# Gathering two graph attentions through rings of eight buffers in place of four, with GpSimd's run-out rounded up to whole rings

## The reference

```
e = leaky_relu(a_src[src] + a_dst[dst], 0.2)
ee = exp(e - segment_max(e, dst)[dst])
alpha = ee / (segment_sum(ee, dst)[dst] + 1e-16)
agg = segment_sum(h[src] * alpha, dst) + b_gat      # then layer norm, top 2 of 4, experts
```

```
h = x @ W;  a_src = (h * att_src).sum(-1);  a_dst = (h * att_dst).sum(-1)
e = leaky_relu(a_src[src] + a_dst[dst], 0.2)
alpha = softmax of e over the edges of one target
x = x + relu(segment_sum(h[src] * alpha, dst) + bias)
x = x + moe(layernorm(x))
```

## Time and profile before

| | |
|---|---|
| median of 3 runs | 5790.37 us (5789.03 to 5790.59) |
| the profiled execution | 5781.05 us, its span 5779.6 us |
| mean granted TensorE clock | 0.797 of full speed |
| busy: PE, DVE, ACT, POOL | 50%, 55%, 28%, 38% of the span |
| stage l1a | about 2215 to 3055 us of the span |
| stage l3a | about 4155 to 5780 us of the span |

### The profile page before, as it was taken

The page is one execution under the profiler, slowest core; times in us unless marked ns, Lnnn a source line. Parts: engine busy times, 40 slices in busy tenths (PEclk is TensorE's granted clock), DMA queues, the critical chain, the costliest instruction groups (busy, mean ns, idle before and its releaser), DMA issues. The chain is left out here.

```text
span 5779.6 us, 67813 instructions
## 1 busy us (share of the span) xinstructions
PE 2908.9 (50%) x15435; PEld 2113.2 (37%) x15474; DVE 3171.6 (55%) x7705; ACT 1642.9 (28%) x2993; POOL 2183.8 (38%) x2146
## 2 busy tenths in 40 slices
PE   0430065895995952566730489958301132343446
PEld 0320064784884841344520234446200111122224
DVE  8876386674776561222224554442455656676663
ACT  0322042773771211223310254322101222222221
POOL 1036212001001526566562100015366656666662
PEclk9999999997996975777865799979655566666678
DMA  0311154543433211111113634432323322332210
GB/s 29 68 32 31 8 195 159 170 131 117 133 95 106 66 57 41 21 25 25 30 23 99 233 128 159 167 98 65 127 71 82 80 68 70 82 79 78 65 43 23
DMA packets 332190, 488.33 MB, mean 84 GB/s; under 512 B 159589, under 2 KB 250259, under 8 KB 330134
## 3 DMA queue, kind: packets, MB, share of 16 engines
q1 hardware_dynamic: 192198, 269.65, 14.9%
q0 software_dynamic: 92304, 177.29, 11.8%
q10 hardware_dynamic: 47552, 39.98, 2.1%
HBM read 375.91 MB, written 137.24 MB: 89 GB/s over the span
## 5 line engine op out<-in xcount | busy, mean ns | idle before, releaser
L2253 POOL DMA_INDIRECT l3a_got<-rows,l3a_idx x928 | 976.6, 1052 | 528.4 <-issue 286.9
L2348 PE MATMUL ps<-l3a_xt,l3a_w 128*128 128x512 f32 (+1 forms) x448 | 268.8, 761 | 739.8 <-ACT l3a_h L2292 492.0
L2652 POOL DMA_INDIRECT l1a_got<-rows,l1a_idx x512 | 510.4, 997 | 318.5 <-issue 159.5
L1581 PE MATMUL ps<-l0a_all_rows,l0a_w 128*128 128x257 f32 x2500 | 556.5, 382 | 28.2 <-DVE l0a_w L1699 28.2
L1581 PEld LDWEIGHTS ps<-l0a_all_rows,l0a_w 128*128 128x128 f32 x2500 | 475.8, 191 | 101.7 <-issue 31.9
L1972 PE MATMUL ps<-l2a_table,l2a_count 128*128 128x512 bf16 x1837 | 411.3, 384 | 61.1 <-DVEq L2067 59.1
L2348 PEld LDWEIGHTS ps<-l3a_xt,l3a_w 128*128 128x128 f32 x448 | 112.0, 276 | 875.6 <-issue 875.4
L2277 ACT ACT_TABLE_LOAD x99 | 127.0, 1283 | 904.5 <-DVEq L2419 583.4
L2686 PE MATMUL ps<-l1a_w,l1a_h 128*128 128x256 f32 x800 | 232.3, 432 | 224.1 <-issue 168.3
L1972 PEld LDWEIGHTS ps<-l2a_table,l2a_count 128*128 128x128 bf16 x1875 | 185.2, 99 | 287.5 <-issue 72.1
L1508 ACT ACTIVATE l0a_low<-ps,l0a_factors x650 | 254.1, 509 | 86.7 <-PE ps L1571 79.1
(11 more groups left out here) (965 smaller groups left out, 6576.1 us busy)
## 6 DMA issues: line engine op xcount, KB each, us to landing
l0a_held<-counts SPq DMA_DIRECT2D x130, 640.0 KB
counts<-count_held SPq DMA_DIRECT2D x13, 3200.0 KB, 9.7
l2a_held<-counts SPq DMA_DIRECT2D x65, 640.0 KB
l3a_got<-rows,l3a_idx POOLq DMA_INDIRECT x928
l_y<-l1a_y_sb ACTq DMA_DIRECT2D x20, 640.0 KB
l2a_table<-rows SPq DMA_DIRECT2D x16, 640.0 KB
l2a_state<-l2a_seen SPq DMA_DIRECT2D x1, 9984.0 KB
l2a_seen<-l2a_state POOLq DMA_DIRECT2D x12, 768.0 KB, 6.0
```

Source lines behind the costliest of these rows:

```text
L1581: ins = pe.matmul(sums_of(n, k, D + 1), w[:, at, k * P:(k + 1) * P], all_rows[:, at, 1:RW], start=(at == 0), stop=False)
L2253: pool.indirect_dma_start(out=got[:, at:at + RW], out_offset=None, in_=rows[:, :], in_offset=bass.IndirectOffsetOnAxis(ap=idx[:, a, k:k + ...
L2348: ins = pe.matmul(ps[:, m, 0:size * P], w1[:, x, k, m * P:(m + 1) * P], xt[:, 0:size, k, :], start=(k == 0), stop=(k == KT - 1))
L2652: pool.indirect_dma_start(out=got[:, at:at + RW], out_offset=None, in_=rows[:, :], in_offset=bass.IndirectOffsetOnAxis(ap=idx[:, a, k:k + ...
```

## The change

`BUFFERS = 4` becomes `RING = 8` in both stages. The two loops run `(total + 7) // 8` times: 14 in l3a (112 blocks, 896 gathers in place of 928) and 8 in l1a (64 blocks as before). The padding behind a table becomes 16 blocks, written by two DMAs. The core of the diff (the same replacements are made in l1a, L2580 to L2656 and L2768):

```
-BUFFERS = 4
+RING = 8
...
-                    total = sp.value_load(s.base_row[0:1, NT:NT + 1], min_val=1, max_val=s.blocks - NT - 2 * SLOTS)
-                    sp.dma_start(s.table[bass.ds(total * (P * SLOTS), P * WIDE), 0].rearrange("(p s) -> p s", s=WIDE), empty[:, :]).then_inc(s.padded, 16)
+                    total = sp.value_load(s.base_row[0:1, NT:NT + 1], min_val=1, max_val=s.blocks - NT - 3 * SLOTS)
+                    for k in range(2):
+                        sp.dma_start(s.table[bass.ds((total + k * SLOTS) * (P * SLOTS), P * WIDE), 0].rearrange("(p s) -> p s", s=WIDE),
+                                     empty[:, :]).then_inc(s.padded, 16)
...
-                    sp.wait_ge(s.padded, 16)
+                    sp.wait_ge(s.padded, 32)
...
-                for a in range(BUFFERS):
+                for a in range(RING):
                     load(a, a)
...
-                with sp.Fori(0, (total + BUFFERS) // BUFFERS) as q:
-                    for a in range(BUFFERS):
+                with sp.Fori(0, (total + (RING - 1)) // RING) as q:
+                    for a in range(RING):
 
                         when(sp, c, gathered[a], (q + 1) * (16 * SLOTS))
                         sp.sem_inc(arrived, 1)
-                        load(q * BUFFERS + (BUFFERS + a), a)
+                        load(q * RING + (RING + a), a)
...
-                with pool.Fori(0, (total + BUFFERS) // BUFFERS) as q:
-                    for a in range(BUFFERS):
+                with pool.Fori(0, (total + (RING - 1)) // RING) as q:
+                    for a in range(RING):
 
                         when(pool, c, idx_in[a], (q + 1) * 16)
-                        when(pool, c, valued, q * (2 * BUFFERS) + (2 * a + 2))
+                        when(pool, c, valued, q * (2 * RING) + (2 * a + 2))
...
-                for a in range(BUFFERS):
+                for a in range(RING):
                     ch(dve.memset(buffer(a), FLOOR))
                     dve.sem_inc(valued, 2)
...
-                    when(dve, c, valued, b * 2 + 2 * BUFFERS)
+                    when(dve, c, valued, b * 2 + 2 * RING)
```

More of the change, by code:

```diff
@@ L2158, in attend_heads_beside_experts @@
         chain_sem, loaded, weights_in, arrived = (sem(n) for n in ("chain", "loaded", "weights_in", "arrived"))
-        idx_in = [sem(f"idx_in_{a}") for a in range(BUFFERS)]
-        gathered = [sem(f"got_{a}") for a in range(BUFFERS)]
+        idx_in = [sem(f"idx_in_{a}") for a in range(RING)]
+        gathered = [sem(f"got_{a}") for a in range(RING)]
         shifted, exped, weighed, valued = (sem(n) for n in ("shifted", "exped", "weighed", "valued"))
@@ L2205, in attend_heads_beside_experts @@
         first_of = lambda g, size: 0 if size == 1 else (g - 1) * G + 1
-        buffer = lambda b: got[:, bass.ds((b % BUFFERS) * (SLOTS * RW), SLOTS * RW)].rearrange("p (s w) -> p s w", w=RW)
+        buffer = lambda b: got[:, bass.ds((b % RING) * (SLOTS * RW), SLOTS * RW)].rearrange("p (s w) -> p s w", w=RW)
         valued_of = lambda b: v[:, bass.ds((b % 2) * (SLOTS * VW), SLOTS * VW)].rearrange("p (s h d) -> p s h d", h=H, d=DH + 1)
@@ L2214, in _ @@
             def _(sp):
-                total = sp.value_load(base_row[0:1, c.NT:c.NT + 1], min_val=1, max_val=blocks - 2 * BUFFERS)
+                total = sp.value_load(base_row[0:1, c.NT:c.NT + 1], min_val=1, max_val=blocks - 2 * RING)
                 def load(b, a):
@@ L2231, in _ @@
                     sp.dma_start(b2[:, :], b_out).then_inc(weights_in, 16)
-                with sp.Fori(0, (total + BUFFERS) // BUFFERS) as q:
-                    for a in range(BUFFERS):
+                with sp.Fori(0, (total + (RING - 1)) // RING) as q:
+                    for a in range(RING):
                         when(sp, c, gathered[a], (q + 1) * (16 * SLOTS))
                         sp.sem_inc(arrived, 1)
-                        load(q * BUFFERS + (BUFFERS + a), a)
-                for a in range(BUFFERS):
-                    when(sp, c, idx_in[a], ((total + BUFFERS) // BUFFERS + 1) * 16)
+                        load(q * RING + (RING + a), a)
+                for a in range(RING):
+                    when(sp, c, idx_in[a], ((total + (RING - 1)) // RING + 1) * 16)
             @block.gpsimd
             def _(pool):
-                total = pool.value_load(base_row[0:1, c.NT:c.NT + 1], min_val=1, max_val=blocks - 2 * BUFFERS)
+                total = pool.value_load(base_row[0:1, c.NT:c.NT + 1], min_val=1, max_val=blocks - 2 * RING)
                 last_node = pool.to_reg(c.N - 1)
-                with pool.Fori(0, (total + BUFFERS) // BUFFERS) as q:
-                    for a in range(BUFFERS):
+                with pool.Fori(0, (total + (RING - 1)) // RING) as q:
+                    for a in range(RING):
                         when(pool, c, idx_in[a], (q + 1) * 16)
-                        when(pool, c, valued, q * (2 * BUFFERS) + (2 * a + 2))
+                        when(pool, c, valued, q * (2 * RING) + (2 * a + 2))
                         for k in range(SLOTS):
@@ L2642, in _ @@
             def _(pool):
-                total = pool.value_load(base_row[0:1, c.NT:c.NT + 1], min_val=1, max_val=blocks - 2 * BUFFERS)
+                total = pool.value_load(base_row[0:1, c.NT:c.NT + 1], min_val=1, max_val=blocks - 2 * RING)
                 last_node = pool.to_reg(c.N - 1)
-                with pool.Fori(0, (total + BUFFERS) // BUFFERS) as q:
-                    for a in range(BUFFERS):
+                with pool.Fori(0, (total + (RING - 1)) // RING) as q:
+                    for a in range(RING):
                         when(pool, c, idx_in[a], (q + 1) * 16)
-                        when(pool, c, freed, q * BUFFERS + (a + 1))
+                        when(pool, c, freed, q * RING + (a + 1))
                         for k in range(SLOTS):
@@ L2765, in _ @@
                 dve.sem_inc(self_free, 2)
-                dve.sem_inc(freed, BUFFERS)
+                dve.sem_inc(freed, RING)
                 dve.sem_inc(emptied, 1)
```

12 lines of the change are left out of this document (6 added, 6 removed).

## The result

The changed kernel took 5893.52 us (5872.36 to 5899.75, 4 runs) against 5790.34 (5789.03 to 5790.59) on the same chip: a ratio of 1.0175, with a 95% interval of 1.0152 to 1.0198. It is 103 us slower. The profiled executions are 5892.2 and 5781.05 us, 111 us apart. The prediction had said 5804, with a range of 5745 to 5842.

What follows compares the result with a forecast made beforehand. DVE, slow while POOL issues without a stop, was taken to bound l3a. Terms 38 + 30 + 2 + 2 + 1 - 37 - 22 = +14 us gave 5795 on the profiled 5781.05, 5804 as median; range 5745 to 5842.

Steps and rivals of the forecast that it cites:

- What bounds the kernel: Both rings: POOL waits for DVE, 233.8 us in l3a and 158.6 in l1a; DVE, with two speeds, bounds l3a.
- slow after some 25 us of issue: Both stages: DVE's steps lengthen once POOL has issued indirect DMAs some 25 us without a stop, until POOL stops.
- Steady state of both rings: nothing.: Both rings once full: DVE's freeing of buffers still sets POOL's starts, so eight buffers change the time by nothing.
- First fill of l3a: Start of l3a: POOL runs eight blocks ahead, not four, with DVE slow meanwhile; +38 us taken.
- the worst pace: First fill of l3a at 24.5 us a block: POOL resumes at 4325.4, +43 us.
- the milder +28: First fill of l3a at 18.3 us a block: POOL stops for block 9 at 4337, +28 us.
- First fill of l1a: Start of l1a: at 21 us a block POOL stops for block 17, +33 us; +30 taken, +34 at 30 us.
- Index loads and padding: Stage starts: four more index loads, +2 us each in l3a and l1a; second padding DMA before table building, +1.
- The ends: Ends of l3a and l1a: last real blocks issued earlier, no dead gathers in l3a; -37 and -22 us.
- it is nothing: Rival, whole kernel: fills and ends cancel or are hidden, +5 us of loads, 5795 us; chance 0.10.
- More buffers feed DVE: Rival, l3a: POOL's stops delay DVE, so its 78.0 us of waits would go, 5717 us; chance 0.03.

Runs made afterwards that it cites:

- four_slow_dve: Kernel before with ring of four and the new run-out, plus six unread DVE memsets in each block of l3a: 5728.7 us.
- eight_slow_dve: Changed kernel with ring of eight, plus six unread DVE memsets in each block of l3a: 5739.41 us.
- four_exact: Kernel before, ring of four in both stages, only the run-out rounded as in the change: 5327.39 us, ratio 0.9994.
- after_again: The changed kernel itself, unedited, on later chips beside the kernel before: 5324.82 us, ratio 0.9999; once more 5327.87 us.
- eight_ahead2: Changed kernel, but POOL at most two blocks ahead of DVE in both stages; against the kernel before 5480.2 us, ratio 1.0289.
- eight_ahead3: Changed kernel, but POOL at most three blocks ahead of DVE in both stages; against the kernel before 5330.58 us, ratio 1.0002.
- the two kernels with pauses: Changed kernel, four blocks ahead, POOL waiting for its own gathers after every second block: 5512.32 us, ratio 1.0353; the text describes only this one.

## Why the prediction was wrong

**What bounds the kernel: right for the first chip, and for it alone.** The stops of POOL, DVE's two speeds and the ready rows were read rightly there. Later DVE has one speed, and POOL waits for it 24.5 us with four buffers and not at all with eight. The prediction took the condition of one measurement for a property of the kernel; nothing in one trace could tell them apart, but it gave no chance to it. Even in that trace its rule, slow after some 25 us of issue, doesn't always hold: 35 us from 5072.24 on pass without a slow block.

**The step that failed: "Steady state of both rings: nothing."** On the first chip the lag grew by 27 us in l1a and 50 in l3a behind the fills. The reasoning (once the ring is full, the same DVE times release POOL) is sound where DVE's times don't depend on POOL's runs: four_slow_dve and eight_slow_dve keep their distance over 112 blocks, to 1.5 us. With slow steps they do depend on them, and the longer fill leaves POOL's runs at another place of DVE's tiles. In l1a the rhythm can be read from POOL's stops, before and after:

```profile
2480.37 0.99 POOL L2652 DMA_INDIRECT l1a_got<-rows,l1a_idx  x1 [6.37 <-DVEq L2819]
2517.70 0.99 POOL L2652 DMA_INDIRECT l1a_got<-rows,l1a_idx  x1 [6.42 <-DVEq L2819]
```

```profile
2427.08 1.00 POOL L2654 DMA_INDIRECT l1a_got<-rows,l1a_idx  x1 [10.35 <-DVEq L2821]
2468.35 0.99 POOL L2654 DMA_INDIRECT l1a_got<-rows,l1a_idx  x1 [10.28 <-DVEq L2821]
```

Three blocks take 37.3 us before and 41.3 after, with the same 31 us of POOL and a stop of 10.3 in place of 6.4. That the place of the runs is the reason is argued from these rows, not shown by a run: no later chip had the slow steps. In l3a not even the rhythm was read, and with executions of the changed kernel up to 27 us apart a part of both drifts may belong to the recorded one alone. The cause of the drifts stays open.

**First fill of l3a: right.** +38 was taken, +36 measured; blocks at 23 to 26 us as at "the worst seen", and POOL goes on at 4378.63, 164 us behind its first gather, where the working at the worst pace had 4325.4 less 4161.5, also 164. So the working at the worst pace, +43, is the one that came out. That the +38 taken, between it and the milder +28, meets the +36 at block 9 is luck in part, since the lag behind the start was +53 at block 7.

**First fill of l1a: mis-sized.** +30 was taken, +34 was the upper bound, about +52 measured (+54 with the start's +2). The sum took 21 us for a block and let POOL stop for block 17. POOL stopped for block 14, and only one block further in DVE's work than before, 59 us behind the 2326.31 of the earlier trace rows: that one block took 49.8 us (2330.92 to 2380.67). The sum priced DVE's own steps and left out that DVE waits for TensorE in a block, whose single matmuls stand 2 to 3.5 us apart; 41.02 of the 49.8 us are such a wait, though its last 11 stand behind the last matmul and no record explains them.

**Index loads and padding:** +2, +2 and +1 predicted; 5 us are what the kernel with eight lags at block 0 of eight_slow_dve. Right in the sum.

**The ends: right.** -37 and -22 predicted, -33 and -25 measured, and the idle time of 25.11 us before L2540 is gone. On the other chips the dead gathers are hidden: four_exact gives 4 us, within what can't be told from none.

The lags of the table add up to -4 + 54 + 27 - 25 + 6 + 36 + 50 - 33 = +111, as they must. The two drifts, 77 us, and 22 of the first fill of l1a are the distance to the forecast of +14. Of the rivals, "it is nothing" gives the right time on the two later chips where the changed kernel ran, though not for its reason: there are no fills to pay. "More buffers feed DVE" has a true core there, since DVE does wait for gathers, but it waits for POOL's pace and not for a buffer, which no ring mends. The rule of the Trainium skill (SBUF — State Buffer, Practical consequences) that a DMA never contends with a compute engine fits the trace of after_again: POOL issues for 1220 us without a stop, and DVE's blocks that wait for nothing take the 7.9 us of the fast stretches. The first chip's traces differ from it as far as DVE's pace goes, whatever the reason.

**What stays open.** Why the first chip had slow steps: steps of 0.7 us and one recorded update in 0.7 us go together there, but a higher rate did nothing on another chip. Whether the recording itself makes the steps slow, and so whether they are in an execution that isn't recorded; this rival is untested. Whether it is the chip or the occasion. And whether a shorter ring or broken runs would help there: eight_ahead2, eight_ahead3 and the two kernels with pauses never met them.

## What to carry to other kernels

Before buying depth, ask which side of the ring waits: where the producer waits for the consumer, more buffers change only when it waits, as with 57 us of POOL's stops that became idle time at the end. Three blocks ahead were enough here, two cost 154 us. And when a trace shows an engine with two speeds for the same instructions, time the kernel on a second chip and once more on the first before explaining a change by it.

## What the runs showed of the hardware that was not expected

The same kernel took 5790 us in the first measurement and 5323 to 5331 on six chips later, with the mean granted clock at 0.797 and 0.813 to 0.817. The mean clock alone does not mark the condition: four_slow_dve, whose l3a is longer for another reason, took 5729 us at 0.791 to 0.796. On the first chip, in long runs of POOL's indirect DMAs, DVE took 24 us for a block of 7.9, TensorE one matmul in 2 to 3.5 us, steps of SP, ACT and DVE that last 0.03 to 0.05 us took 0.7, and the trace held a tenth of the semaphore increments. A trace of the other chips held up to 376 increments in 10 us in l3a with none of this.
